# Second attention of a four-layer kernel: context load ahead of the stacking transfers, rounded rows stacked first, batches 0 and 1 prepared two mixed batches sooner

## The reference

```python
x = x + tanh(g_xattn[0]) * L0_xattn(layernorm(x), ctx, ctx, mask, ...)   # 32 heads of 128
x = x + tanh(g_ffn[0])   * L0_ffn(layernorm(x), ...)                     # base product, routed LoRA
x = x + tanh(g_xattn[1]) * L1_xattn(layernorm(x), ctx, masks, ...)       # patches, 8 heads of 8
x = x + tanh(g_ffn[1])   * L1_ffn(layernorm(x), ...)                     # top 2 of 8 experts
```

```python
q = einsum('ed,bdw->bew', Wq, qp) + bq[:, None]
k = einsum('ed,bdw->bew', Wk, qp) + bk[:, None]
val = einsum('ed,bdw->bew', Wv, vp) + bv[:, None]
scores = einsum('bhdi,bhdj->bhij', qh, kh) / sqrt(dh)      # then mask, softmax
o = gelu(einsum('bhij,bhdj->bhdi', attn, vh))
out = (einsum('de,bew->bdw', Wo, o) + bo[:, None]) * masks
```

## Time and profile before

| | |
|---|---|
| three runs | 1085.51, 1089.72, 1091.14 us; median 1089.72 |
| the profiled execution | 1085.18 us |
| its span, first to last instruction | 1083.4 us, mean granted TensorE clock 0.908 |
| busy share of the span | TensorE 86%, VectorE 57%, GpSimd 38%, ScalarE 30% |
| second attention, TensorE's granted clock (708 to 882 us) | 0.75 |

### The profile page before, as it was taken

How to read it: one execution, slowest core, us unless ns; L and a number is a source line. 1 busy time by engine, 2 the same in 40 slices (tenths; PEclk the granted TensorE clock), 3 DMA queues, 4 the chain that set the end, 5 groups by cost and what they waited for, 6 DMA issues and landing times.

```text
span 1083.4 us, 13787 instructions
## 1 busy us (share of the span) xinstructions
PE 932.4 (86%) x4739; PEld 750.8 (69%) x4739; DVE 618.1 (57%) x1073; ACT 322.5 (30%) x575; POOL 408.2 (38%) x418
## 2 busy tenths in 40 slices
PE   4899999999998999999999979868878878757990
PEld 4777778877777778778777657647767775345770
DVE  5775764565752665753757656754644735855344
ACT  4332142141231141331321311133433537322220
POOL 3641531431520523423415242454433422717540
PEclk9899999999998999999999999966876967659995
DMA  8020210110200110200200211112222104133437
GB/s 280 10 78 1 68 39 10 39 40 30 78 1 12 41 38 30 79 1 10 78 1 1 70 60 39 30 30 79 80 81 86 50 21 182 68 107 117 136 136 253
DMA packets 42446, 70.12 MB, mean 65 GB/s; under 512 B 7240, under 2 KB 14984, under 8 KB 42256
## 3 DMA queue, kind: packets, MB, share of 16 engines
q1 hardware_dynamic: 37264, 56.95, 16.3%
q0 software_dynamic: 3680, 12.06, 3.4%
q10 hardware_dynamic: 1440, 0.24, 0.1%
HBM read 52.59 MB, written 10.22 MB: 58 GB/s over the span
## 4 chain that ended last, share of the span: by engine, by line
PE 70%; issue 8%; DVE 7%; POOL 7%; SPq 3%; DMA 3%; ACT 2%; ACTq 1%; POOLq 0%; DVEq 0%
PE ps L1351 18%; PE ps L1353 16%; PE ps L1352 16%; PE ps L1440 5%; POOL k_blk L586 5%; PE ps L1448 4%; PE ps L1456 2%; PE ps L1577 2%; SPq L416 1%; SPq L424 1%; PE ps L1565 1%; DVE at_lo L1006 1%; PE ps L1680 1%; DMA rows_in<-h_rows,gather_i 1%; ACT at_hi L741 1%
## 5 line engine op out<-in xcount | busy, mean ns | idle before, releaser
L512 POOL TENSOR_TENSOR q_t<-rot_a,rot_b 128x512 f32<-128x512 f32 x64 | 82.6, 1291 | 146.2 <-DVE rot_b L933 146.2
L1351 PE MATMUL ps<-wo_hi,at_hi 128*128 128x512 f32 x256 | 108.8, 425 | 18.7 <-DVE at_lo L1006 11.9
L931 DVE TENSOR_TENSOR rot_a<-ps,cos 128x512 f32<-128x512 f32 x80 | 55.3, 692 | 113.5 <-PE ps L1353 113.5
L1351 PE MATMUL ps<-xt_hi,wq_hi 128*128 128x512 f32 x256 | 107.9, 421 | 0.2 <-issue 0.2
L1353 PE MATMUL ps<-xt_hi,wq_lo 128*128 128x512 f32 x256 | 101.0, 395 | 0.0
L1352 PE MATMUL ps<-xt_lo,wq_hi 128*128 128x512 f32 x256 | 100.6, 393 | 0.0
L1353 PE MATMUL ps<-wo_hi,at_lo 128*128 128x512 f32 x256 | 100.4, 392 | 0.0
L1352 PE MATMUL ps<-wo_lo,at_hi 128*128 128x512 f32 x256 | 100.0, 391 | 0.0
L741 ACT ACTIVATE at_hi<-ps 128x512 fp32r<-128x512 f32 x64 | 38.2, 597 | 189.1 <-PE ps L1456 189.1
L1011 DVE TENSOR_TENSOR X<-ps,X 128x512 f32<-128x512 f32 x64 | 44.2, 691 | 84.9 <-PE ps L1353 84.9
L730 ACT ACTIVATE ps<-ps 128x512 f32<-128x512 f32 x64 | 37.2, 582 | 175.8 <-PE ps L1440 175.8
(11 more groups left out here) (221 smaller groups left out, 2164.9 us busy)
## 6 DMA issues: line engine op xcount, KB each, us to landing
wq_raw<-in_wq SPq DMA_DIRECT2D x8, 1024.0 KB, 5.5
wo_raw<-in_wo SPq DMA_DIRECT2D x8, 1024.0 KB, 5.2
w_raw<-in_we SPq DMA_DIRECT2D x8, 1024.0 KB, 5.7
y_in<-y_rows SPq DMA_DIRECT2D x16, 256.0 KB, 5.3
X<-in_x SPq DMA_DIRECT2D x4, 512.0 KB, 13.3
wk_raw<-in_wk SPq DMA_DIRECT2D x8, 256.0 KB, 3.0
q_t<-in_ctx_t SPq DMA_DIRECT2D x2, 1024.0 KB, 10.2
wv_raw<-in_wv SPq DMA_DIRECT2D x4, 512.0 KB, 4.4
```

The source lines that it names most:

```text
L512: nc.gpsimd.tensor_tensor(dst, rot_a[:, r % 2, :], rot_b[:, r % 2, :], ALU.add).then_inc(rope_ok, 1)
L931: nc.vector.tensor_tensor(heads(rot_a[:, r % 2, :]), heads(bank), bcast(cos[:, :], 4), ALU.mult)
L1351: nc.tensor.matmul(dst, w_hi, x_hi, start=start and k == 0, stop=False)
```

## The change

Four edits go together.

1. SyncE loads the context of a batch ahead of that batch's stacking transfers.
2. `stack` waits for H only, sends the four rounded parts of the keys first, and waits for R just ahead of the two remainders.
3. GpSimd runs R(b + 1) behind K(b), where it ran R(b + 2) behind K(b).
4. Batches 0 and 1 are normalised, projected, evicted, rounded and, for batch 0, stacked and written to `k_blk` two turns of the mixed stage sooner; K(0) and R(1) stand on GpSimd within the mixed stage.

```diff
             def stack(b):
-                sp.wait_ge(qkl_ok, CREDIT + b + 1)
+                sp.wait_ge(qkh_ok, CREDIT + b + 1)
                 if b >= 1:
                     sp.wait_ge(kb_ok, CREDIT + H1 * b)
-                for g in range(2):
-                    rows = slice(E1 + g * half, E1 + (g + 1) * half)
-                    for n, part in enumerate((qk_hi, qk_lo, qk_hi)):
+                for n, part in ((0, qk_hi), (2, qk_hi), (1, qk_lo)):
+                    if n == 1:
+                        sp.wait_ge(qkl_ok, CREDIT + b + 1)
+                    for g in range(2):
+                        rows = slice(E1 + g * half, E1 + (g + 1) * half)
                         sp.dma_start(k3[n * half:(n + 1) * half, g, :].bitcast(F32), part[rows, :].bitcast(F32)).then_inc(k3_in[g], 16)
...
             for b in range(2, B):
-                stack(b)
                 sp.wait_ge(vc_mm, CREDIT + b - 1)
                 load_ctx(b, b % 2)
+                stack(b)
...
-            mixed(0, 0)
-            for b in range(1, B):
-                mixed(b, b % 2)
-                row_scale(2, b - 1, (b - 1) % 2)
-                if b == B - 3:
-                    gp.wait_ge(qkh_ok, CREDIT + 1)
-                    lo_part(qk_lo[:, :], qk_raw[:, :], qk_hi[:, :], qkl_ok)
-            row_scale(2, B - 1, 1)
...
             gp.wait_ge(late_in, 16 * N_LATE)
-            remainder(1)
-            for b in range(B):
+            mixed(0, 0)
+            for b in range(1, B):
+                mixed(b, b % 2)
+                row_scale(2, b - 1, (b - 1) % 2)
+                if b == B - 5:
+                    remainder(0)
+                if b == B - 3:
+                    keys(0, 0, KT)
+                if b == B - 2:
+                    keys(0, KT, H1)
+                    remainder(1)
+            row_scale(2, B - 1, 1)
+
+
+            for b in range(1, B):
                 keys(b)
-                if b + 2 < B:
-                    remainder(b + 2)
+                if b + 1 < B:
+                    remainder(b + 1)
...
-            for b in range(B - 1):
-                mix(b, b % 2, True)
-            round_qk(0)
-            mix(B - 1, 1, False)
-            round_qk(1)
+            for b in range(B):
+                if b == B - 3:
+                    round_qk(0)
+                if b == B - 1:
+                    round_qk(1)
+                mix(b, b % 2, b < B - 1)
...
-                if b == B - 3:
+                if b == B - 5:
                     ve.wait_ge(maskb_in, 16 * B)
                     rows(0, 0, p_w)
                     kept(0, 0)
-                if b == B - 2:
+                if b == B - 4:
                     evict(0, 0, 7)
                     rows(1, 1, p_w)
                     kept(1, 1)
-            evict(1, 1, 7)
+                if b == B - 3:
+                    evict(1, 1, 7)
...
-                if b >= B - 2:
-                    pe.wait_ge(qk_ev, CREDIT + b - B + 2)
-                    proj(b - B + 2, b % 2, p_w, 7)
+                if B - 4 <= b < B - 2:
+                    pe.wait_ge(qk_ev, CREDIT + b - B + 4)
+                    proj(b - B + 4, b % 2, p_w, 7)
```

More of the change, by code:

```diff
@@ L577, in remainder, with keys @@
                 lo_part(qk_lo[:, :], qk_raw[:, :], qk_hi[:, :], qkl_ok)
-            def keys(b):
-                for u in range(H1):
+            def keys(b, first=0, end=H1):
+                for u in range(first, end):
                     patch, g = divmod(u, 2)
```

## The result

The changed kernel took 1021.99 us (median of four runs, 1021.69 to 1025.34); the kernel before took 1087.62 beside it (1084.62 to 1091.14). The ratio is 0.9402, with a 95% interval of 0.9364 to 0.9441: 65.6 us less by these medians. The forecast was 1025, with a range of 1015 to 1044. The profiled execution took 1021.97 us; against the 1085.18 of before that is 63.2 us less, for 62.6 in the prediction's sum.

The account below looks back on a forecast made before the run. One serial loop of waits in the second attention, 25.1 us a period, was taken as the bound. Savings of 58.2 + 4.4 = 62.6 us from 1085.18 gave 1022.6; half of 4.5 us added made 1025, range 1015 to 1044.

Parts of the forecast that it names:

- the prediction's sum: Whole kernel: 58.2 us less in the second attention plus 4.4 us less at its start, 62.6 us.
- One serial loop: Second attention: K, S, context, TensorE and ScalarE up to H, and R wait for each other, 25.1 us a period.
- The three loops that are left: Second attention, per batch after the change: GpSimd and SyncE 13.2 us, ScalarE and SyncE 11.5, TensorE 16.35, setting the period.
- Context first: SyncE's queue: the context is issued while the queue stands idle behind K; 3.0 us of transfer leave the loop.
- rival 2: Second attention: H waits for S, which lands too late, and K follows; period 20.8 us, time 1053; chance 0.10.
- The start: Batches 0 and 1 prepared sooner: batch 1 starts 5.2 + 0.2 us earlier, 1 us off for the clock; 4.4 us less.
- the wait of VectorE for X of batch 7: End of mixed stage: VectorE's statistics wait for X until 706.3; first row maximum of batch 0 comes at 708.1.
- The clock: Second attention: granted clock 0.50 up to about 717 to 722, then 1.00 to the end.
- rival 3: Second attention: the clock falls once in each batch; six batches, every second one hit, cost 17 us: 1042; chance 0.05.
- upward range for a slow recovery: Batch 1: the clock recovers in this batch only, as in the 12 us of 830 to 842; +5 us.
- The half spread: Whole kernel: the profiled execution lay 4.5 us below the median of four times; half of that was added to the forecast.

## Why the prediction was right

- **One serial loop.** Right. R ahead of K closes it: put back into the changed kernel it gives 20 to 21 us a batch on GpSimd; put right in the kernel before, by itself, it gives 47 us. The period read from the rows (25.1 us for a true 25.9) was the sum of that loop.
- **The three loops that are left, TensorE's the largest.** Right: 16.36 us a batch for 16.35, 97.3 us for six batches for 97.2. GpSimd's and SyncE's loop (13.2) and ScalarE's and SyncE's (11.5) have slack: GpSimd waits for keys and for H, TensorE for neither. That slack is why the context's place and the stacking order each count nothing in the changed kernel.
- **Context first.** The prediction counted it as 3.0 us taken out of the loop and gave it no price of its own. In the changed kernel it is worth nothing: the loops come apart without it. Alone it gives 36 us, by the mechanism of rival 2 (37.1 us from batch 1 to batch 7, for 30.6 in its sum, since the batches came to 19.7 us on average and not 20.8). The two edits on one loop don't add: 36 alone and 47 alone, and 60 to 66 with all.
- **The start.** The sum was right (4.4 us forecast; first row maximum of batch 1 at 724.84, forecast 729.07 - 4.4 = 724.7), and so was the wait of VectorE for X of batch 7 (statistics at 707.61 for 706.3, first row maximum of batch 0 at 709.07 for 708.1). The 1.0 to 1.3 us too many come from t_b of batch 5, which started 1.9 us late, at 692.22, where I had kept the 690.28 of before. What was wrong is whose gain it is. I gave the 4.4 us to the early preparation, since H(2) doesn't wait. Without that preparation the time is 0.5 us more by the medians and 2.5 us by the profiled executions, not 4.4: R behind K alone lets K(0) start before H(1), and batch 0 starts at 704.38. Batch 1 then starts 0.5 us late, and the rest is half clock within it. I had weighed the preparation against the kernel before, and not against the kernel with the other three edits.
- **The clock.** It recovered near 719, within the 717 to 722 named, and did not fall in dense work: rival 3 did not come true in the changed kernel, whose one wait of 0.76 us in each batch left the clock at 1.00 from 720 to 842. The Trainium skill (TensorE: Matmul & The Clock Gate, section A second HAM failure mode: psum-queue depth-cycling) tells of a kernel that idled briefly between its groups of matmuls and swung between the two levels; this trace does not agree. The 5 us of upward range for a slow recovery was too small for one of the two profiles (11 us).
- **The median.** The half spread that I added (2.4 us) wasn't needed: four runs of the changed kernel lie within 3.7 us, and its profiled execution on their median. Six more runs of it later spread over 14.7 us, so the close fit owes something to chance.

## What to carry to other kernels

Where several engines wait for each other, follow one item round through each in-order queue before pricing an edit: an instruction that waits closes a loop for all that is queued behind it, and moving it behind them can be worth more than its own length many times over. Savings within one loop don't add up; price each edit against the kernel that already has the others, and look for the next loop, which takes over. Work moved sooner into an idle stretch still stands ahead of something: name that. Here it was the addition to X of batch 7, which the next stage had to wait for. And read the periods of an experiment as well as its time, since a time can fit a theory that its trace does not show.

## What the runs showed of the hardware

- The length of TensorE's recovery varies between executions of one program. With nearly the same first matmul behind the idle stretch of 10.4 us (710.62 and 711.32) the granted clock rose to 1.00 at about 719 in one execution and at about 740 in the other, in which TensorE was busy throughout from 724 to 740. The cost was 10.6 us at the first row maximum of batch 7 (822.14 and 832.71). The three kernels without the early preparation show it too: behind a wait of 3.1 to 4.5 us ahead of batch 1 the clock was back at 1.00 at 729, 731 and 739.
- A short wait of TensorE can go with a fall of the clock or not, and its length does not tell which. The 0.76 us in every batch of the changed kernel left it at 1.00. In the kernel with R behind K alone, 0.76 and 0.55 us with 0.47 us of work between them were followed by 0.50 from 760 to 768. In the kernel with the context first alone, 1.53 us (to 765.10) and 0.23 us (to 766.93) left it at 1.00. No experiment was made on this, and the cause is open.
- Beside GpSimd's keys, VectorE's TENSOR_SCALAR operations took longer and its other ones did not. In the changed kernel `keep` (128x512) took 0.94 us beside the keys and 0.47 to 0.48 without them, and a 128x16 `alpha` 1.08 us at 695.08 for 0.23 at 690.42; the normalise of the kernel before shows the same. The row maxima (0.68 us), the subtractions (0.69), `t_b` (0.75) and `z_w` (0.29) took as long beside the keys as without them.
